# Masked cross-attention of 16 heads: the first score pass on two halves of the array's rows, two units in a row

## The reference

```
q = x @ Wq.T + bq                    # 4 x 512 x 256
k = context @ Wk.T + bk              # 4 x 1601 x 256
v = context @ Wv.T + bv
scores = einsum('bhtd,bhcd->bhtc', q, k) / sqrt(d)     # 16 heads, d = 16
...
out = softmax(scores) @ v ; out @ Wo.T + bo
```

## Time and profile before

| | us |
|---|---|
| median of three runs | 3843.1 |
| lowest, highest | 3841.2, 3844.5 |
| profiled execution, span from the first to the last instruction | 3829.6 |
| TensorE busy with matmuls | 3401.9 |
| VectorE, ScalarE, GpSimd busy | 2159.4, 2034.7, 745.3 |

### The profile page before, as it was taken

The page is one execution under the profiler, slowest core; times in us unless marked ns, Lnnn a source line. Parts: engine busy times, 40 slices in busy tenths (PEclk is TensorE's granted clock), DMA queues, the critical chain, the costliest instruction groups (busy, mean ns, idle before and its releaser), DMA issues.

```text
span 3829.6 us, 52360 instructions
## 1 busy us (share of the span) xinstructions
PE 3401.9 (89%) x18396; PEld 1770.7 (46%) x18396; DVE 2159.4 (56%) x3463; ACT 2034.7 (53%) x4490; POOL 745.3 (19%) x768
## 2 busy tenths in 40 slices
PE   5899999988689989997899799989987979987997
PEld 3333333325432323332697322323326956687996
DVE  6767676736757777873402477767743033264333
ACT  2566666763236666775333266667772322244664
POOL 2211111003635331000302141210002010022332
PEclk8999999999779999998899799999998989999998
DMA  8132424105664443211874655644208521042554
GB/s 194 42 103 61 106 57 110 26 14 187 178 182 124 101 111 82 45 24 46 267 231 154 185 152 118 171 112 103 77 10 285 186 78 69 1 143 92 184 186 167
DMA packets 314686, 456.02 MB, mean 119 GB/s; under 512 B 66315, under 2 KB 234195, under 8 KB 312251
## 3 DMA queue, kind: packets, MB, share of 16 engines
q1 hardware_dynamic: 233206, 285.70, 27.5%
q0 software_dynamic: 29568, 104.65, 8.2%
q10 hardware_dynamic: 51653, 62.32, 5.8%
HBM read 292.46 MB, written 153.91 MB: 117 GB/s over the span
## 4 chain that ended last, share of the span: by engine, by line
PE 67%; DVE 13%; DMA 8%; ACT 4%; POOL 3%; issue 3%; SPq 1%; ACTq 0%; another core or an unknown queue 0%; POOLq 0%; DVEq 0%
PE pv L1325 14%; PE m L1289 11%; PE s L1311 9%; DVE mxp L1172 9%; PE h L2811 5%; PE y L2819 5%; PE h L2385 4%; PE y L2394 4%; PE y L1791 2%; PE s L1771 2%; PE s L1256 2%; DMA sums<-rc 2%; ACT e_t L1403 1%; DMA ot<-sums 1%; PE m L1333 1%
## 5 line engine op out<-in xcount | busy, mean ns | idle before, releaser
L1172 DVE TENSOR_REDUCE mxp<-m 128x1 f32<-128x802 f32 x1536 | 1447.8, 987 | 526.9 <-PE m L1289 523.2
L1403 ACT ACTIVATE e_t<-s 128x512 f32<-128x512 f32 (+1 forms) x2496 | 1340.3, 599 | 552.0 <-PE s L1311 532.9
L1289 PE MATMUL m<-kaug,qaug 97*128 97x401 bf16 x3072 | 811.6, 347 | 97.5 <-DVE mxp L1172 51.6
L1311 PE MATMUL s<-qaug,kaug 100*128 100x512 bf16 (+1 forms) x2496 | 859.4, 386 | 34.1 <-ACT e_t L1403 29.0
L1325 PE MATMUL pv<-e_t,v 128*32 128x512 f32 (+1 forms) x4992 | 670.3, 609 | 0.2
L1311 PEld LDWEIGHTS s<-qaug,kaug 100*128 100x128 bf16 (+1 forms) x2496 | 229.4, 99 | 733.8 <-ACT e_t L1403 519.6
L1289 PEld LDWEIGHTS m<-kaug,qaug 97*128 97x128 bf16 x3072 | 273.4, 99 | 506.7 <-DVE mxp L1172 265.2
L127 POOL TENSOR_TENSOR rstd<-rstd,mhalf 128x16 f32<-128x16 f32 (+2 forms) x9 | 24.2, 2690 | 1150.8 <-DVE rstd L120 1150.8
L2881 ACT ACTIVATE ez<-h,b 128x128 f32<-128x128 f32 x440 | 120.1, 388 | 159.7 <-PE h L2811 159.7
L1325 PEld LDWEIGHTS pv<-e_t,v 128*32 128x32 f32 (+1 forms) x4992 | 98.6, 108 | 214.9 <-ACT e_t L1403 161.3
L2272 DVE SCALAR_TENSOR_TENSOR y<-y,b 128x256 f32<-128x256 f32 x39 | 16.6, 425 | 303.0 <-PE y L2394 303.0
(11 more groups left out here) (377 smaller groups left out, 3616.2 us busy)
## 6 DMA issues: line engine op xcount, KB each, us to landing
w<-in_L_w POOLq DMA_DIRECT2D x78, 1024.0 KB, 5.4
w<-in_L_w SPq DMA_DIRECT2D x24, 1024.0 KB, 12.7
xregion<-zero ACTq DMA_DIRECT2D x10, 2056.0 KB, 12.2
kaug<-kparts SPq DMA_DIRECT2D x16, 1200.8 KB
kaug<-kready SPq DMA_DIRECT2D x32, 600.4 KB
kaug<-kready SPq DMA_DIRECT2D x16, 1200.8 KB
vn<-values SPq DMA_DIRECT2D x8, 1536.0 KB
values<-p_vb ACTq DMA_DIRECT2D x21, 512.0 KB
```

The costliest lines, as they stand in the source:

```text
L1172: dve.tensor_reduce(a.mxp[:, u.g % 2, half, n:n + 1], a.m_slot[u.m % 2][:].rearrange("p (a n) -> p a n", a=2)[:, :, 0:PIECE + 1], AX.XY, A ...
L1289: m = pe.matmul(slot[:, 512 * k:512 * k + PIECE + 1], a.qaug[0:R_MAX, u.g, j, P * qc:P * qc + P], a.kaug[0:R_MAX, u.g, j, k0:k0 + PIECE + ...
L1311: pe.matmul(slot[0:KW[u.k], :], a.kaug[0:R_ALL, u.g, u.j, P * u.k:P * u.k + KW[u.k]], a.qaug[0:R_ALL, u.g, u.j, :], start=True, stop=True) ...
L1403: act.activation(a.e_t[0:KW[u.k], e % 2, u.j, :], a.s_slot[u.s % 3][0:KW[u.k], :], ACT.Exp).then_inc(s_free.sem, 1)
```

## The change

The head's columns are divided anew. `kaug` and `qaug` get a second index for the side: heads 0 and 1 of a group stand on the low side, heads 2 and 3 on the high side. On the low side rows 0 to 47 hold three of the six products, row 48 the mask, rows 49 to 96 the other three, rows 97 to 99 the maxima. On the high side rows 64 to 111 and 112 (mask) take the place of rows 0 to 48, rows 0 to 47 the other three products, 48 to 50 the maxima, and rows 51 to 63 are zeros. The first pass now takes three products only, 48 rows and the mask: rows 0 to 48 for a head of the low side, rows 64 to 112 for one of the high side.

- A unit is one matmul of each side, over 49 rows, with the same 401 keys, for two heads; the results go to the two halves of the same `m_slot`, and the reduction gives two maxima of 401 values. There are still 32 units of two matmuls a group, and `maxima` now yields after every second one: two units follow each other directly. `MAX_STEPS` is 18 instead of 34.
- The second pass uses 100 rows on the low side and 113 on the high side, in one matmul as before.
- The peak takes the maximum over four pieces of keys instead of two.
- Stores are three DMAs as before. A group's q is fetched by four DMAs instead of one, its k by four instead of one (eight instead of two in layer 1), the mask row by two, the maxima are written by six instead of three, and the rows filled at the start of a layer by six DMAs instead of two (layer 0: eight instead of three). In layers 1 and 2 the GpSimd fills a second stretch of `fill`.

```diff
+LOW = Rows(0, slice(0, 2), 0, TRIPLE, TRIPLE + 1, 2 * TRIPLE + 1, 0, 2 * TRIPLE + 4)
+HIGH = Rows(1, slice(2, 4), HALF, HALF + TRIPLE, 0, TRIPLE, HALF - TRIPLE - 3, HALF + TRIPLE + 1)
+SIDES = (LOW, HIGH)
...
-MAX_STEPS = 2 * HG * QC + 2
+MAX_STEPS = HG * QC + 2
...
             self.add("max", b=b, g=g, k=i)
             if self.to_turn:
                 self.add("turn", **self.to_turn.pop())
-            yield
+            if i % 2:
+                yield
...
+def fetch_heads(sp, to, src, g, by, dmas):
+
+    h0, h1 = HG * HD * g, HG * HD * (g + 1)
+    for side in SIDES:
+        for half, row in enumerate((side.lead, side.rest)):
+            of = src[half, h0:h1, :, :].rearrange("(h d) s k -> (d s) h k", d=HD)
+            sp.dma_start(to[row:row + TRIPLE, side.at, g, :, :], of[:, side.heads, :]).then_inc(by.sem, DMA)
...
-            for k in range(3):
-                sp.dma_start(a.qaug[R_MAX + k:R_MAX + k + 1, u.g, :, :].rearrange("a j (c q) -> a (j c) q", q=P),
-                             a.tm[16 * k:16 * k + 16, :]).then_inc(td.sem, DMA)
+            peaks_sp(sp, a, u.g, td)
...
-            dve.tensor_reduce(a.mxp[:, u.g % 2, half, n:n + 1],
+            dve.tensor_reduce(a.mxp[:, u.g % 2, piece, :].rearrange("p (a n) -> p a n", a=2)[:, :, n],
                               a.m_slot[u.m % 2][:].rearrange("p (a n) -> p a n", a=2)[:, :, 0:PIECE + 1],
-                              AX.XY, ALU.max).then_inc(m_free.sem, 1)
+                              AX.X, ALU.max).then_inc(m_free.sem, 1)
...
-            for k in range(2):
-                k0 = PIECE * (2 * half + k)
-                m = pe.matmul(slot[:, 512 * k:512 * k + PIECE + 1], a.qaug[0:R_MAX, u.g, j, P * qc:P * qc + P],
-                              a.kaug[0:R_MAX, u.g, j, k0:k0 + PIECE + 1], start=True, stop=True)
+            for i, side in enumerate(SIDES):
+                lo, hi = side.lead, side.mask + 1
+                m = pe.matmul(slot[:, 512 * i:512 * i + PIECE + 1], a.qaug[lo:hi, i, u.g, j, P * qc:P * qc + P],
+                              a.kaug[lo:hi, i, u.g, j, k0:k0 + PIECE + 1], start=True, stop=True)
             m.then_inc(m_full.sem, 1)
...
-            pe.matmul(slot[0:KW[u.k], :], a.kaug[0:R_ALL, u.g, u.j, P * u.k:P * u.k + KW[u.k]],
-                      a.qaug[0:R_ALL, u.g, u.j, :], start=True, stop=True).then_inc(s_full.sem, 1)
+            side, j = divmod(u.j, HG // 2)
+            n = SIDES[side].every
+            pe.matmul(slot[0:KW[u.k], :], a.kaug[0:n, side, u.g, j, P * u.k:P * u.k + KW[u.k]],
+                      a.qaug[0:n, side, u.g, j, :], start=True, stop=True).then_inc(s_full.sem, 1)
```

More of the change, by code:

```diff
@@ L80, in fence @@
                 eng.wait_ge(sem, value)
-RUNS = ((0, 0, 3), (3, 1, 2), (5, 2, 1))
+RUNS = dict(k=((0, 0, 0, 1), (0, 1, 0, 2), (1, 0, 0, 3)), q=((0, 0, 1, 2), (0, 2, 2, 1), (1, 0, 0, 3)))
+N_RUNS = 3
+PART_AT = dict(k=(0, 1, 2), q=(2, 1, 0))
 def store_parts(eng, kind, to, src, sem):
[L91 to L94, removed]
+    for half, slot, first, many in RUNS[kind]:
+        eng.dma_start(to[half, :, slot:slot + many, :], src[:, first:first + many, :]).then_inc(sem, DMA)
 def flat2(a):
@@ L420, in prepare_close @@
     return [(kn.sema(n).sem, kn.sema(n).base) for n in names]
-R_MASK = 16 * 6
-R_MAX = R_MASK + 1
-R_ALL = R_MAX + 3
 HG = 4
+HALF = P // 2
+TRIPLE = 3 * 16
+@dataclass
+class Rows:
+    at: int
+    heads: slice
+    lead: int
+    mask: int
+    rest: int
+    peak: int
+    gap: int
+    every: int
+LOW = Rows(0, slice(0, 2), 0, TRIPLE, TRIPLE + 1, 2 * TRIPLE + 1, 0, 2 * TRIPLE + 4)
+HIGH = Rows(1, slice(2, 4), HALF, HALF + TRIPLE, 0, TRIPLE, HALF - TRIPLE - 3, HALF + TRIPLE + 1)
+SIDES = (LOW, HIGH)
+FILL = 16
 NG = H // HG
@@ L603, in lay_out @@
         v = self.project(0, (), "v")
-        for n, _ in enumerate(self.maxima(0, 0, alone=True)):
-            if n % 2:
-                next(v, None)
+        for _ in self.maxima(0, 0, alone=True):
+            next(v, None)
         for _ in v:
@@ L739, in head_attention @@
         if ready:
[L740 removed]
+            a.fill = sb("fill", [FILL, 2 * S2], BF16)
         else:
@@ L932, in head_ready_sp, with fetch_turned @@
     piece = lambda t: t.rearrange("(c t h i) s k -> c t h i s k", c=DC, t=2, h=H // DC)
+    def fetch_turned(src, g, by):
+        c, h, r = g // (NG // DC), HG * (g % (NG // DC)), TRIPLE // 2
+        for side in SIDES:
+            for half, row in enumerate((side.lead, side.rest)):
+                for t in range(2):
+                    of = piece(src[half])[c, t, h:h + HG, :, :, :].rearrange("h i s k -> (i s) h k")
+                    sp.dma_start(a.kaug[row + r * t:row + r * t + r, side.at, g, :, :], of[:, side.heads, :]).then_inc(by.sem, DMA)
+                    n_of(by.sem.name)
     splits = [x for x in plan.units if x.kind in ("q", "k")]
@@ L987, in head_ready_sp @@
             sp.wait_ge(filled.sem, filled.at(1))
-            for t, r, h, n in ((a.kaug, R_MAX, R_ALL - R_MAX, S2), (a.qaug, R_MASK, 1, T)):
-                sp.dma_start(t[r:r + h, :, :, :].rearrange("p g j n -> p (g j) n"),
-                             a.fill[0:h, 0:n].rearrange("p (a n) -> p a n", a=1).to_broadcast([h, H, n])).then_inc(rows.sem, DMA)
-                n_of("rows")
+            fill_rows(sp, a, True, rows)
+            a.dmas["rows"] = 6
         elif u.kind == "prep_loads":
@@ L2926, in first_loads_act @@
     act.wait_ge(filled.sem, filled.at(1))
-    for t, r, h, src in ((a.kaug, R_MAX, R_ALL - R_MAX, a.fill[0:R_ALL - R_MAX, 0:S2]), (a.qaug, R_MASK, 1, a.fill[0:1, 0:T]),
-                         (a.kaug, R_MASK, 1, a.fill[0:1, S2:2 * S2])):
-        act.dma_start(t[r:r + h, :, :, :].rearrange("p g j n -> p (g j) n"), spread(src)).then_inc(rows.sem, DMA)
+    fill_rows(act, a, False, rows)
 def first_consts_act(kn, a):
```

127 lines of the change are left out of this document (65 added, 62 removed).

## The result

The changed kernel takes 3943.8 us (median of 4 runs, 3936.7 to 3955.9) against 3843.8 for the kernel before (3841.2 to 3849.8): a ratio of 1.026, with a 95% interval of 1.0241 to 1.0279. It is slower, as forecast, and inside the range; but 100 us slower, where the forecast said 38.

A forecast was written before the change was run, and what follows sets the result against it. TensorE, busy 89% of the span, was taken to bound, only 9 us above ScalarE and VectorE; +15 from the attentions' stretches and +23 from SP's DMAs on the 3843 median gave 3881 us, range 3790 to 3970.

The forecast's parts named there:

- Step 1: In m's matmuls on TensorE: a unit's two row halves run together, 0.17 us instead of 0.35.
- Step 2: On TensorE around each pair: switching to row halves costs 0.10 us each way, leaving 2.8 us saved a stretch.
- The rival of free switches: Row halves on TensorE need no emptying: 3814 us, or 3803 with SP's issues half hidden; chance 0.32, cheap switches included.
- dearer switches: Rival: switches to row halves on TensorE cost 0.20 us each, 3994 us; chance 0.11 together with SP late.
- no overlap: Rival: a unit's two matmuls on TensorE still take 0.35 us, 4108 us in all; chance 0.07.
- SP late: Rival: in 24 renewing stretches rc comes late and VectorE stands, 58 us, 3939; chance 0.11 together with dearer switches.
- Step 3: Pairs fill both m buffers, so TensorE waits for VectorE: 5.2 us a stretch in layers 1 and 2, 4.2 in layer 0.
- Step 4: Two iterations a stretch without any m cost 0.2 us each; then the stretches of all layers are summed.
- Together +15: Sum over the attentions' stretches in us: +31 in layers 1 and 2, -12 and -4 in layer 0.
- step 5: SP's additional DMA issues at the very start, layer 0's batch starts and the starts of layers 1 and 2: together 23 us.
- I take nothing: In renewing stretches, layer 1's ten extra DMAs (4.8 us) ahead of the z and rc moves were booked at no cost.

The follow-up runs named there:

- experiment 7: The changed kernel with both matmuls of a unit on rows 0 to 48 of the low side: 4243.6 us, 1.1037 of the kernel before.
- experiment 1: The changed kernel with its halved rows, but units one by one again as before: 3853.4 us, 1.0027 of the kernel before.
- experiment 9: The changed kernel with the turn moved out of the gap between a pair's units and made its own step: 3933.2 us, 1.0224 of the kernel before.
- experiment 2: The kernel before with two units in a row, whole rows and no new DMAs: 3942.8 us, ratio 1.0261.
- experiment 5: The changed kernel with two units ahead of each pv and the left-over units singly after the second s: 3925.9 us, 1.0218 of the kernel before.
- experiment 4: The changed kernel with each s issued twice where only s stand between two pairs: 3915.0 us, 1.0192 of the kernel before.
- experiment 3: The kernel before with q, k, mask row and peak transfers split as in the change, fills as before: 3854.2 us, ratio 1.0023.

## Why the prediction was right in sign and wrong in size

**Step 1 (overlap) was right.** The trace has the two matmuls of a unit 3 to 4 ns apart, and experiment 7 prices the overlap at 0.34 a pair. The Trainium skill's 4 ns (TensorE: Matmul & The Clock Gate, Part 3) agrees.

**Step 2 (switches) was right** at 0.10 each way, in the changed kernel's rows and in experiment 1's. The rival of free switches fell with it, and so did "dearer switches" and "no overlap". "SP late" at 3939 stands next to the measured 3944 by chance: its mechanism was not there (see below).

**Step 3 (the second unit waits) was right where it was walked, and incomplete.** The places with three s between two pairs cost what was said. But the walk left out the turn, which stands inside a pair and waits 0.93; experiment 9 gives it 0.8 to 1.2 a stretch in layers 1 and 2. Layers 1 and 2 at the full clock came out at 40.6 instead of 40.1.

**Step 4's "Together +15" is the step that failed, first in layer 0.** "In layer 0 six stretches hold projections between the units, so VectorE keeps up: 2.8 less 0.8 left over, 6 x -2.0 = -12; eight others -4." Three of the six went from 60 to 61.6 us at the full clock, and the other three from 50.2 to 51.7 up to 53.3 to 54.1. With single units (experiment 1) they were 60.1 to 60.4 and 49.9 to 51.7, no better than before; over pairs of whole rows (experiment 2, 62.2 to 62.5) the halves gave 0.6 to 0.9. VectorE did keep up, as the step had it: in the first of them all units of a pair but the one at the turn go 0.18 apart. But ScalarE did not, and the walk had no wait for it. The kernel before and then the changed kernel, at the same place:

```profile
167.88 0.51 PE L1289 MATMUL m<-kaug,qaug 97*128 97x401 bf16 x2
168.68 0.39 PE L1311 MATMUL s<-qaug,kaug 100*128 100x512 bf16 x1 [0.29 <-ACT ks L1375]
```

```profile
179.44 0.60 PE L1358 MATMUL s<-qaug,kaug 100*128 100x512 bf16 x2
181.02 0.39 PE L1358 MATMUL s<-qaug,kaug 113*128 113x512 bf16 x1 [0.98 <-ACT ks L1422]
```

Projections and s share three buffers, which ScalarE empties (`ks` is its copy of a projection of keys). Before, a unit stood between two s, and the next s went 0.80 after its start instead of 0.35. With the units taken together, three s follow each other, and the third goes 1.58 after the first instead of 0.44. By the starts of all matmuls in that stretch, s behind s wait 2.6 us in six places, where before two s behind a unit waited 0.9 and no s behind an s. With the 0.93 at the turn that is 2.6 of the 3.6 us between the forecast's -2.0 and the measured +1.6; the other 1.0 was not settled. It is the wait that experiment 5 shows among four s: a unit between two s hides it.

Of the eight others, the steady ones went from 39.4 to 40.1 at the full clock where the step had 38.9 (its own terms give 39.1), and the three with the output product from 42.5 to 46, or to 43.9 where the clock stayed full (experiment 4). Layer 0 gave +31 where -9 was forecast, transfers included: 40 of the 87 us by which this execution lies above the forecast's +38.

**The granted clock had no term.** Of its two levels, 1.2 and 2.4 GHz, TensorE spent 120 us more at the lower in the three attentions, and layer 0's start fell from 0.85 to 0.78. Experiment 4 got 29 us back with more matmuls in the waits. It was in reach of the profile of before only in part: layer 0's start already stood at 0.85 and ran on waits, so that making TensorE's work shorter there was a question to ask. The fall in the middle of stretches that stood at 0.99 was not.

**The transfers (step 5) were over-priced, as far as they were measured:** 16.5 without the fills, where experiment 3 has 10. What the fills cost in the end is open. At layer 1's start the sum came near by luck (8.2 later, 6.5 forecast): the fills took 7.0 more where 3.0 was forecast, the keys' DMAs 0.6 where 2.9 was, and of the 8.2 only 2.4 lay on the path. In turn "I take nothing" for the sums behind a renewal was wrong in one place: the first stretch of layer 1. The reciprocal waited 2.2 us there before, 5.0 with pairs and 8.8 with single units. It was this one stretch, and not the 24 that the rival had.

**Put together:** the pairs cost 100 (experiment 2), the transfers some 10 (experiment 3), and the halves gave 1.9 a stretch at the full clock in layer 1 where step 2 had 2.8, for in the places that wait for VectorE a shorter pair only waits longer. Over 42 stretches the 1.9 would be 80, and the total shows no gain from the halves. At least some 29 of what is missing went with the lower clock (experiment 4); how the rest divides among the clock, layer 0's smaller gain and the fills is not shown. The forecast weighed the same three against each other, but booked the halves' gain in all 42 stretches and at the full clock.

## What to carry to other kernels

Dividing a matmul's rows saves half its time only if the mode switches are shared: here 0.10 each way against 0.17 saved, so a single unit between whole-array matmuls gains nothing, and only a pair, or a unit beside an operation in a divided mode, does. But a pair fills both buffers that the next engine empties at 0.93 each; the order that shares a switch is the order that makes TensorE wait, and the two must be walked together, with every other user of those buffers (here the turn), and with the other engines' buffers too: what stood between two s hid ScalarE's time. When a change makes the bounding engine's work shorter without making the kernel's path shorter in proportion, ask what the granted clock does with it.

## What the runs showed of the hardware

- In layer 1's attentions the granted clock was 0.99 with TensorE 95% busy (m on 97 rows), 0.91 at 94% (m on 49 rows, one matmul after the other) and 0.96 at 89% (two of 49 rows together). What of the work sets it was not tested by itself.
- Two matmuls of 49 rows on different halves of the array start 3 to 4 ns apart, and the next unit's 0.18 us after them; on the same rows a pair of units costs 0.34 us more.
- Between the whole array and m's halves a change costs about 0.10 us: going in 0.10 (0.32 against 0.22), and again on leaving (0.28 from a single unit to the next s in experiment 1, 1307.31 to 1307.59, where the two units of a free pair go 0.18 apart).
- A transfer's issue can hold its engine: `sums<-rc` took 6.54 us to issue on ScalarE's queue with 2 MB of zeros ahead of it and the renewal's keys issued 5 us before those, and 0.33 in the kernel before with the same zeros and the keys 14 us before them. Everything behind it on ScalarE stood.
